# Mixture of experts on one core: gates applied at the PSUM eviction, expert rows added by the scatter itself, and a combine phase that reads two sums

## The reference, cut to what matters

```python
x = layernorm(x + attention(x))                      # B, T, D = 4, 1024, 256; 16 heads
raw_gate = softmax(x @ gate)                         # 16 experts
mask = one_hot(top_k(raw_gate, 3)).sum(axis=2)
gate_topk = mask * raw_gate
gate_topk = gate_topk / max(sum(abs(gate_topk)), 1e-12)
hidden = relu(einsum('btd,edh->bteh', x, W1) + b1)   # 256 -> 512
expert_out = einsum('bteh,ehd->bted', hidden, W2) + b2
x = layernorm(x + einsum('bte,bted->btd', gate_topk, expert_out))
```

## Time and profile before

| | us |
|---|---|
| median of 3 runs | 1911.62 (1911.14 to 1917.54) |
| time of the profiled execution | 1915.52 |
| its span, first to last instruction | 1913.8 |

### The profile page before, as it was taken

The page is one execution under the profiler, slowest core; times in us unless marked ns, Lnnn a source line. Parts: engine busy times, 40 slices in busy tenths (PEclk is TensorE's granted clock), DMA queues, the critical chain, the costliest instruction groups (busy, mean ns, idle before and its releaser), DMA issues. The chain is left out here.

```text
span 1913.8 us, 33436 instructions
## 1 busy us (share of the span) xinstructions
PE 1725.6 (90%) x9587; PEld 1286.1 (67%) x9588; DVE 1390.2 (73%) x3237; ACT 752.6 (39%) x1633; POOL 1202.2 (63%) x1128
## 2 busy tenths in 40 slices
PE   5489999999999999999999999998679999999930
PEld 4356666766766676676676667654359999999930
DVE  3358888888888888988888888855964444444448
ACT  3124444444445444444544444444432222222225
POOL 2138778777877777887786787651445555555544
PEclk9679999999999999999999999998569999999975
DMA  9856556755745775565666557506602222222255
GB/s 311 274 166 182 160 166 191 196 154 155 193 139 177 208 209 152 172 171 160 189 203 182 165 144 196 157 1 207 214 30 70 71 69 71 71 69 71 69 189 186
DMA packets 165567, 294.72 MB, mean 154 GB/s; under 512 B 18736, under 2 KB 59440, under 8 KB 165440
## 3 DMA queue, kind: packets, MB, share of 16 engines
q1 hardware_dynamic: 152624, 262.51, 46.5%
q0 software_dynamic: 10752, 29.37, 4.9%
q10 hardware_dynamic: 2064, 1.31, 0.2%
HBM read 190.12 MB, written 102.76 MB: 153 GB/s over the span
## 5 line engine op out<-in xcount | busy, mean ns | idle before, releaser
L735 ACT ACTIVATE prob<-b_ps 128x512 f32<-128x512 f32 (+3 forms) x768 | 354.4, 488 | 367.8 <-PE b_ps L572 267.8
L499 POOL TENSOR_TENSOR acc<-acc,prob 128x1024 f32<-128x1024 f32 (+1 forms) x192 | 352.3, 1835 | 6.4 <-POOL acc L499 3.6
L571 PE MATMUL b_ps<-q,k 128*128 128x512 f32 (+3 forms) x768 | 296.6, 390 | 11.8 <-DMA q<-mrow 7.4
L472 POOL TENSOR_TENSOR roped<-rot 128x512 f32<-128x512 f32 x128 | 174.6, 1364 | 183.6 <-DVE rot L858 182.8
L564 PE MATMUL a_ps<-k,q 128*128 128x512 f32 (+3 forms) x768 | 267.1, 385 | 19.4 <-DMA k<-scratch_hilo 9.0
L840 DVE CUSTOM_DVE_ANT_0 masked<-a_ps,causal 128x128 bf16<-128x128 f32 (+3 forms) x512 | 237.3, 479 | 59.3 <-PE a_ps L564 51.7
L653 PE MATMUL y_ps<-prob,v_sb 128*64 128x512 f32 (+3 forms) x1536 | 276.6, 496 | 0.0
L1551 DVE TENSOR_SCALAR hT<-h_ps,b1T 128x128 f32<-128x128 f32 x448 | 126.1, 344 | 191.2 <-PE h_ps L1470 179.3
L572 PE MATMUL b_ps<-q,k 65*128 65x512 f32 (+3 forms) x768 | 264.8, 348 | 0.0
L888 DVE RECIPROCAL inv<-inv 128x128 f32<-128x128 f32 x256 | 232.2, 929 | 8.5 <-ACT inv L776 6.2
L477 POOL TENSOR_TENSOR lo<-roped,hi 128x512 fp32r<-128x512 f32 x128 | 176.9, 1382 | 85.9 <-ACT hi L748 85.9
(11 more groups left out here) (263 smaller groups left out, 2524.8 us busy)
## 6 DMA issues: line engine op xcount, KB each, us to landing
q<-scratch_hilo SPq DMA_DIRECT2D x192, 256.0 KB, 4.6
k<-scratch_hilo SPq DMA_DIRECT2D x192, 256.0 KB, 5.2
scratch_hilo<-hi SPq DMA_DIRECT2D x64, 512.0 KB, 3.9
scratch_hilo<-lo SPq DMA_DIRECT2D x64, 512.0 KB, 4.5
w_sb<-scratch_wsplit SPq DMA_DIRECT2D x32, 512.0 KB, 3.6
w<-in_L_ffn_W_dram SPq DMA_DIRECT2D x32, 512.0 KB, 9.6
got<-scratch_ys SPq DMA_DIRECT2D x32, 384.0 KB, 6.1
wv_sb<-scratch_wsplit SPq DMA_DIRECT2D x16, 512.0 KB, 6.1
```

Source lines behind the costliest of these rows:

```text
L499: nc.gpsimd.tensor_tensor(sums, old, probs(q), ALU.add).then_inc(m["sum_p"], 1)
L571: nc.tensor.matmul(out, k1[s][:, h, js], q1[s][:, h, qs], start=True, stop=False, skip_group_check=True)
L735: nc.scalar.activation(probs(q)[:, h, :], b_ps[:, h, 0:w], ACT.Exp).then_inc(exp_done[h], 1)
```

## The change

The two columns of work that combine did on each of the three rows, multiplying by the gate and adding, move into the expert phase.

- **Rows of `xn` grow** from 256 to 272 numbers (1024 to 1088 bytes): the 16 gates of the token stand ahead of its features. SP writes the gates there, one DMA of 128x32 runs of 16 numbers (64 bytes), after the gates are done and behind the weights (L1038 of the kernel after). VectorE waits for it (`r_gst`) ahead of the decoding, since that reuses `tmp`. `wts` goes.
- **Two sums in DRAM**, `sum0` and `sum1`, 4096 rows and 128 spare rows each. SP first writes zeros to all of `sum1` and to the spare rows of `sum0` (L1036), and later stores the residual rows (with the gated `b2`) into `sum0`, 1 MB for each batch when GpSimd has added its biases (L1043). GpSimd waits for all six DMAs (`sums_in`) ahead of the first scatter.
- **Experts.** The gather brings the gates with the rows. ScalarE multiplies at the eviction to `y` by the gate column of the tile's expert (a register load for the column ahead of each). The scatter of tile t adds to `sum(t mod 2)` in DRAM (`compute_op=ALU.add`), and waits for scatter t-2. `dst_i` is now the token's row, or a spare row. `XIN` goes from 4 to 8, since the gates in `xin` are read late; the gather still runs 4 tiles ahead (`AHEAD`). `XIN` is also what one pass of the hardware loops handles: 8 tiles, 13 passes, and a tail of 8.
- **Combine** reads two rows for each token (8 MB) in groups of 4, 8, 8, 8 and 4 tiles, all ten loads issued at once. GpSimd adds the two (one instruction for each group), VectorE takes the moments, ScalarE applies scale and shift, and SP stores group by group.

```diff
-XIN = 4
+XIN = 8
+AHEAD = 4
+SUMS = 2
@@ routing, sync
+            sp.wait_ge(m["r_zero"], 1)
+            some = S["zeros"][:].rearrange("p (t d) -> p t d", t=1)
+            for i in range(SUMS):
+                rows = dram[f"sum{i}"].rearrange("(t p) d -> p t d", p=P)[:, TILES if i == 0 else 0:TILES + 1, :]
+                sp.dma_start(rows, some.broadcast_to([P, rows.shape[1], D])).then_inc(S["sums_in"], 16)
+            sp.wait_ge(m["r_g32"], 1)
+            sp.dma_start(dram["xn"].rearrange("(t p) c -> p t c", p=P)[:, :, 0:E_], tmp[:]).then_inc(m["r_gst"], 16)
+            first = dram["sum0"].rearrange("(t p) d -> p t d", p=P)
+            for g in range(GROUPS):
+                sp.wait_ge(m["r_bbadd"], LG * (g + 1))
+                half = S["x1a"] if g < 2 else S["x1b"]
+                sp.dma_start(first[:, g * LG:(g + 1) * LG, :], half[:, g % 2 * LG:g % 2 * LG + LG, :])\
+                    .then_inc(S["sums_in"], 16)
@@ routing, vector
-                V.tensor_tensor(wts[:], top[:, :, 0:TOPK], bc(red[:, 1, :], TOPK), ALU.mult)
...
             dve.wait_ge(m["r_inv"], BATCHES)
+            dve.wait_ge(m["r_gst"], 16)
@@ experts, gpsimd
-            for t in range(XIN):
+            for t in range(AHEAD):
                 gather(t)
+            pool.wait_ge(S["sums_in"], 16 * (SUMS + TILES // TB))
             for t in range(SLOT_TILES):
-                if t + XIN < SLOT_TILES:
+                if t + AHEAD < SLOT_TILES:
 
                     pool.wait_ge(m["m_xtr"], done(t))
-                    gather(t + XIN)
+                    gather(t + AHEAD)
                 pool.wait_ge(m["m_ytaken"], done(t))
+                if t >= SUMS:
+                    pool.wait_ge(ys_st[(t - SUMS) % 2], 16 * ((t - SUMS) // 2 + 1))
                 pool.indirect_dma_start(
-                    out=dram["ys"], out_offset=bass.IndirectOffsetOnAxis(ap=dst_i[:, t:t + 1], axis=0),
-                    in_=y[:, t % 2, :], in_offset=None).then_inc(ys_st[t % 2], 16)
+                    out=dram[f"sum{t % SUMS}"], out_offset=bass.IndirectOffsetOnAxis(ap=dst_i[:, t:t + 1], axis=0),
+                    in_=y[:, t % 2, :], in_offset=None, compute_op=ALU.add).then_inc(ys_st[t % 2], 16)
@@ experts, scalar
+                e = act.value_load(etile[0:1, bass.ds(t, 1)], min_val=0, max_val=E_ - 1)
                 act.wait_ge(m["m_y"], done(t))
...
-                nc.scalar.activation(y[:, s, :], yo_ps[:, s, 0:D], ACT.Copy).then_inc(m["m_ytaken"], 1)
+                nc.scalar.activation(y[:, s, :], yo_ps[:, s, 0:D], ACT.Copy, scale=xin[:, place, bass.ds(e, 1)])\
+                    .then_inc(m["m_ytaken"], 1)
@@ combine
-    GROUPS = TILES // GRP
+    SIZES = (4, 8, 8, 8, 4)
...
+            for g in range(GROUPS):
+                for i in range(SUMS):
+                    sp.dma_start(got[i][:, rows(g), :],
+                                 dram[f"sum{i}"].rearrange("(t p) d -> p t d", p=P)[:, rows(g), :]).then_inc(ld[g], 16)
...
+                pool.wait_ge(ld[g], 32)
+                nc.gpsimd.tensor_tensor(got[0][:, rows(g), :], got[0][:, rows(g), :], got[1][:, rows(g), :], ALU.add)\
+                    .then_inc(m["c_added"], 1)
```

More of the change, by code:

```diff
@@ L923, in routing_phase @@
     w1, w2, b1T = S["w1"], S["w2"], S["b1T"]
-    src_i, dst_i, wts, gT, etile, ident = (S[k] for k in "src_i dst_i wts gT etile ident".split())
+    src_i, dst_i, gT, etile, ident = (S[k] for k in "src_i dst_i gT etile ident".split())
     with ExitStack() as ctx:
@@ L1034, in _ @@
         def _(pool):
+            pool.memset(S["zeros"][:], 0.0).then_inc(m["r_zero"], 1)
             pool.memset(tri[:], -1.0).then_inc(m["r_const"], 1)
@@ L1387, in _ @@
             V.tensor_scalar(src_i[:], place, -float(HOT), 0.0, ALU.add, ALU.max)
[L1388 to L1390 removed]
+            link(V.scalar_tensor_tensor(out=more, in0=place, scalar=0.5, in1=unused[:], op0=ALU.is_lt, op1=ALU.mult))
             link(V.tensor_scalar(src_i[:], src_i[:], TILES - 1, None, ALU.bitwise_and))
             link(V.tensor_copy(which, src_i[:]))
[L1393 removed]
+            link(V.scalar_tensor_tensor(out=place, in0=which, scalar=float(P), in1=row, op0=ALU.mult, op1=ALU.add))
+            V.tensor_copy(src_i[:], place)
+            V.tensor_tensor(dst_i[:], place, more, ALU.add)
 def expert_phase(nc, A, dram, S):
@@ L1523, in step @@
                     take_x(t + 2, s % 2)
-                take_y(t, s % 2)
+                take_y(t, s)
             take_x(0, 0)
@@ L1573, in combine_phase @@
 def combine_phase(nc, A, dram, S, out):
-    wts = S["wts"]
-    GROUPS = TILES // GRP
-    AHEAD = 4
-    SUMS_V = 2
-    SUMS_P = GRP - SUMS_V
+    SIZES = (4, 8, 8, 8, 4)
+    ENDS = [sum(SIZES[:g + 1]) for g in range(len(SIZES))]
+    GROUPS = len(SIZES)
     with ExitStack() as ctx:
@@ L1582, in sb @@
             return ctx.enter_context(nc.sbuf_tensor(name, shape, dt))
-        got = sb("got", [P, AHEAD, GRP, TOPK * D], F32)
+        got = [sb(f"got{i}", [P, TILES, D], F32) for i in range(2)]
         stats = sb("stats2", [P, TILES, 6], F32)
@@ L1631, in _ @@
+                nc.gpsimd.tensor_tensor(got[0][:, rows(g), :], got[0][:, rows(g), :], got[1][:, rows(g), :], ALU.add)\
+                    .then_inc(m["c_added"], 1)
         @block.scalar
         def _(act):
-            def scale_rows(g):
-                act.wait_ge(ld[g % AHEAD], 16 * GRP * (g // AHEAD + 1))
-                for k in range(TOPK):
-                    for i in range(SUMS_V, GRP):
-                        rows = got[:, g % AHEAD, i, k * D:(k + 1) * D]
-                        t = g * GRP + i
-                        nc.scalar.activation(rows, rows, ACT.Copy, scale=wts[:, t, k:k + 1])\
-                            .then_inc(m["c_scaled"], 1)
@@ L1699, in scales @@
                 dve.wait_ge(m["c_std"], g + 1)
-                ts = slice(g * GRP, (g + 1) * GRP)
-                root, first, a, rs, shift = (r[:, i, ts] for i in range(5))
+                root, first, a, rs, shift = (r[:, i, rows(g)] for i in range(5))
                 link(V.reciprocal(first, root))
                 link(V.tensor_tensor(a, first, first, ALU.mult))
-                link(V.scalar_tensor_tensor(out=root, in0=mv[:, ts, 1], scalar=EPS, in1=a, op0=ALU.add, op1=ALU.mult))
+                link(V.scalar_tensor_tensor(out=root, in0=mv[:, rows(g), 1], scalar=EPS, in1=a, op0=ALU.add, op1=ALU.mult))
                 link(V.tensor_scalar(a, root, -0.5, 1.5, ALU.mult, ALU.add))
                 link(V.tensor_tensor(rs, first, a, ALU.mult))
-                V.scalar_tensor_tensor(out=shift, in0=mv[:, ts, 0], scalar=-1.0, in1=rs, op0=ALU.mult,
+                V.scalar_tensor_tensor(out=shift, in0=mv[:, rows(g), 0], scalar=-1.0, in1=rs, op0=ALU.mult,
                                        op1=ALU.mult).then_inc(m["c_rs"], 1)
-            sums(0)
+            moments(0)
             for g in range(GROUPS):
-                moments(g)
                 if g + 1 < GROUPS:
-                    sums(g + 1)
+                    moments(g + 1)
                 scales(g)
@@ L1742, in scratch @@
 def scratch(nc):
-    shapes = {"xsplit": [B, P, 2 * DK * T], "wsplit": [PAIRS + PAIRS // 2, P, 2 * DK * 256], "hilo": [2, 2, P, 2, T], "xn": [NTOK, D],
-              "ys": [PLACES * NTOK + SLOT_TILES * P, D]}
+    shapes = {"xsplit": [B, P, 2 * DK * T], "wsplit": [PAIRS + PAIRS // 2, P, 2 * DK * 256], "hilo": [2, 2, P, 2, T], "xn": [NTOK, E_ + D]}
+    shapes.update({f"sum{i}": [NTOK + P, D] for i in range(SUMS)})
     return {k: nc.dram_tensor(f"scratch_{k}", v, F32, kind="Internal").ap() for k, v in shapes.items()}
```

93 lines of the change are left out of this document (26 added, 67 removed).

## The result

The changed kernel takes 1894.31 us (median of 4 runs, 1892.5 to 1896.71), the kernel before beside it 1912.05: ratio 0.9902, interval 0.9878 to 0.9926. It is faster by about 1%, where 1924 and slower was predicted. The time is that of the first rival, "nothing is refetched", 1888 (1881 to 1895), at the upper end of its bounds.

The account below looks back on a forecast made before the run. PE was taken to bound the expert loop, DMA then VectorE and GpSimd combine. Combine -24.8, routing +0.5, scatter +1.0 and loop refetching +36 sum to +12.7 us on 1911.6: 1924 us, slower, range 1882 to 1940.

Parts of the forecast that it names:

- nothing is refetched: Rival, expert loop: the instruction buffer holds three packets or more, 3.73 us a tile stays; 1888 us (1881 to 1895), chance 0.30.
- Experts, the loop's length: Expert loop: PE's doubled body is refetched at each of 12 jumps back, +36 us (13 to 48); forecast's chance 0.55.
- If the buffer holds only two: Expert loop: with two packets kept and a body across three, every jump back waits for a fetch; a guess, +36 us.
- The price of a jump: Expert loop: PE's wait for a fetch at each jump back, taken as 3.0 us, between 1.1 and 4.0.
- Combine: Last phase: less arithmetic and fewer loads shorten it from 73.1 to 48.3 us, -24.8 us (bounds -32 and -20).
- ScalarE, once it is behind, ends groups 2, 3 and 4 at 37.2, 40.8 and 42.6: Combine: end times of ScalarE's scale-and-shift applications, in us from the first load's issue, at 3.6 us for 8 tiles.
- Scatter with addition: Expert phase: adding in DRAM lands 1 us later than the plain scatter, paid once at the end, +1.0 us.
- The scatter becomes the bound: Rival, expert loop: beyond 6.8 us to landing, each further us costs 56 us; at 8.0 us, 1955 us; chance 0.10.
- Routing: Before the experts: zeros, gates and residual stores barely touch the first gather, +0.5 us (0 to 3).
- a run costs as much as one of 1024 bytes: Routing: assumed cost of each of the gates' 4096 64-byte runs, making 13 us more of DMA, until 1395.

Follow-up runs that it names:

- e1_body8: The kernel before with one edit: hardware loop passes of TensorE, VectorE and ScalarE handle 8 tiles instead of 4; 1911.47 us, ratio 1.0000.

## Why the prediction was wrong, step by step

- **Experts, the loop's length: wrong, and this alone turned the sign.** Predicted +36 us (13 to 48), measured 0 (within 3, `e1_body8`): the longer body crosses more packets than the old one, but the buffer keeps them, up to 16 tiles. The failing step is "If the buffer holds only two". The rows showed only that the old body's packets stay, which bounds the buffer from below; the one argument for exactly two, that packets are fetched late, says nothing on how many are kept. The price of a jump was taken too high as well: 3.0 us, for the 1.7 that PE and the 2.1 that its weight loads stood idle; the expert phase grew by 2.1 us for each jump (the medians by 5.5 us for two, interval 2.7 to 8.2).
- **Combine: direction right, the gain over-estimated.** -19.6 for -24.8 us, just short of the -20 that was given as the bound. That bound stood for slow additions (2.8 us per 1024 columns); they took 2.33, so that it nearly fits is chance. The loads went as laid out: GpSimd's additions start at 5.6, 12.0, 18.0 and 24.1 us, for 5.6, 12.0, 18.4 and 24.8. What failed is "ScalarE, once it is behind, ends groups 2, 3 and 4 at 37.2, 40.8 and 42.6": it ends them at 41.1, 46.6 and 50.1. Two terms were missing, the waits of tiny VectorE instructions and the queueing of the root, and one was mis-sized, the applications. The waits of VectorE for GpSimd's wide additions made the second group's scales ready at 31.5 instead of 27.2, +4.3 (3.8 in its own instructions, the rest from the group before). The trace before had it in small: a tiny `L1705` took 162 ns as a rule and 648 at most. And the root that queues behind the applications makes 5.5 us a group, where 3.6 was laid out, +3.2 to the last application; 0.4 of the 1.9 for each group is the applications themselves, 0.51 us a tile for 0.45. The queueing of the root is read from the timeline; the runs that moved roots ahead changed other things too. From the last application to the end it took 3.4 us instead of 5.7, -2.3, perhaps because the store before was already out. In sum +5.2.
- **Scatter with addition: right.** +1.0 predicted, 1.4 to 1.7 measured, nothing in the loop, since 3.8 us to the landing are far from the 6.8 that it bears. The rival "The scatter becomes the bound" begins at 6.8. On the DMA share, the Trainium skill ("Collectives: The Full Stack", The bandwidth ceiling) led to 0.34; measured is 0.45. Doubling the plain scatter's half of the share does not give that; the packets double too, since adding rows go one by one (20,012 packets in the loop for 10,029). How much of the share is reading and how much the smaller packets, no run separates. It cost nothing either way.
- **The drain behind the last scatter** has 1.1 us more that the sum did not have.
- **Routing: within its bounds.** From the last batch's moments to the first gather it was 101.6 us before (1310.12 to 1411.69) and 101.5 with plain scatters, where +0.5 was predicted. In the changed kernel's profile it was 100.2, by a wait for the gate's matmul of 2.75 us instead of 4.00. Of the nine traces with the changed routing six have the shorter time and three the longer, all four with the old routing the longer; what decides is not known, so the 1.3 us are not counted to the change. VectorE did not wait for the gates: they were down at 1382, and it asked at 1401. The rest of the 3.1 us by which the experts start earlier is the end of attention, which moved between 1305 and 1311 us over all traces, with the old routing and the new. That "a run costs as much as one of 1024 bytes" was far too much: see below.
- **The sum with what was measured:** -19.6 + 1.4 + 1.1 + 0 = -17.1 us on 1911.6, 1894.5, for 1894.31. The first tiles of the experts take 0.5 us more on top, and runs of one kernel spread by some 4 us, so the agreement to 0.2 us is luck. In the pair of profiled spans, -19.6 + 2.5 for the drain + 0.5 for the first tiles of the experts - 3.1 for the earlier start is the 19.7.
- The mistake in judgement: 0.55 on a guess that no row of either side spoke for, in a term larger than all others together.

## What to carry to other kernels

A longer hardware loop is free as long as its body stays in the buffer, and the trace of a kernel tells whether it does: count the instruction queue's packets inside the loop. Here twice and four times the body of before was free, and seven times cost about 2 us for each jump back. An adding scatter costs time only where someone waits for its landing; two targets in turn keep it off the path. When work of two engines is merged into fewer, wider instructions, look for small instructions on VectorE beside wide ones on GpSimd, and for a small instruction queued on one engine behind a batch that belongs to the step before.

## What the runs showed of the hardware

- TensorE's instruction buffer keeps a loop body of 832 matmuls and weight loads (no refetch, no stall) and not one of 1456: 9 packets again and 1.6 to 1.8 us of idle PE for each jump back.
- An adding indirect scatter of 128 rows of 1024 bytes: 1.59 us on GpSimd for 0.99, landing 3.8 us after its start, twice the packets. In a chain, the next one starts 4.6 to 4.7 us later.
- Runs of 64 bytes are cheap to store for the DMA engines. The gates' 4096 runs went out between stretches of 1 KB packets; DMA of the kernel after, 1375.6 to 1380.8 us:

```profile
DMA packets 4703, 0.85 MB, mean 164 GB/s; under 512 B 4128, under 2 KB 4703, under 8 KB 4703
```

  16 engines have 83 us of time in 5.2 us. The 575 packets of 1 KB take about 42 ns each, by 387 GB/s in the 5 us before (1370 to 1375), so 24 us; the other 59 us for 4128 small packets make about 14 ns each, an estimate, a third of a 1 KB packet. From issue to landing that DMA took 20.8 us, most of it behind the zeros in the same queue. The penalty that the Trainium skill names below 512 bytes ("DMA: Bandwidth & Descriptors", Specifications) does not make such a run dearer than a long one.
- A tiny VectorE instruction that meets a GpSimd addition takes as long as what is left of the addition: with two SBUF inputs up to 2.52 us for 0.16, a `TENSOR_SCALAR` with one up to 4.35 us for 0.17. Moments (`BATCH_NORM_STATS2`, 0.34 us a tile) and the reciprocal ran beside the additions undisturbed.
